# Three steps of the eighth pair put in another order: turning v, the coefficients of x, and a copy of half an expert

## The reference

```python
x = x + _L0_conv_ref(_gn(x), ...)   # shared + two chosen experts
x = x + _L1_conv_ref(_gn(x), ...)   # window attention + depthwise conv of v, projected
```

## Time and profile before

| | |
|---|---|
| median of three executions | 763.06 us (760.45 to 766.43) |
| profiled execution, its own time | 761.66 us |
| its span, first to last instruction | 759.7 us |
| PE busy | 645.3 us, 85% |
| DVE busy | 565.1 us, 74% |
| ACT busy | 453.1 us, 60% |
| POOL busy | 188.5 us, 25% |
| mean granted TensorE clock | 0.963 of full speed |

### The profile page before, as it was taken

One profiled execution on the slowest core, in us unless ns is written; L12 is line 12 of the kernel. 1 busy time (PEld: TensorE's weight loads), 2 busy tenths in 40 slices (PEclk: granted clock), 3 DMA queues, 4 the chain that ended last, 5 costly groups with the idle time before them and its releaser, 6 DMA issues.

```text
span 759.7 us, 18623 instructions
## 1 busy us (share of the span) xinstructions
PE 645.3 (85%) x6926; PEld 388.0 (51%) x6926; DVE 565.1 (74%) x1124; ACT 453.1 (60%) x758; POOL 188.5 (25%) x295
## 2 busy tenths in 40 slices
PE   5426759899989899999999899999999898889892
PEld 3412324655556464656555565646566566444430
DVE  3842656888888888988888888889888977332692
ACT  1123555768676776867686767768676852355451
POOL 4042133140404223131404042231312101000182
PEclk9997868999999999999999999999999999999997
DMA  8433183555646574746556464747452242465194
GB/s 329 180 132 98 59 223 108 174 158 153 184 129 200 145 206 147 213 128 200 160 151 189 128 199 144 215 138 210 134 168 86 82 147 72 139 222 181 20 257 167
DMA packets 53871, 121.13 MB, mean 159 GB/s; under 512 B 10131, under 2 KB 26646, under 8 KB 53782
## 3 DMA queue, kind: packets, MB, share of 16 engines
q1 hardware_dynamic: 41814, 78.87, 32.9%
q0 software_dynamic: 8800, 28.45, 15.3%
q10 hardware_dynamic: 3168, 12.62, 4.3%
HBM read 70.58 MB, written 40.93 MB: 147 GB/s over the span
## 4 chain that ended last, share of the span: by engine, by line
PE 47%; ACT 25%; issue 12%; DVE 6%; DMA 5%; POOL 1%; ACTq 1%; POOLq 1%; SPq 0%; DVEq 0%
PE g L1067 10%; PE g L1085 7%; ACT y L518 6%; PE t L1135 4%; PE g L1095 4%; PE g L1263 4%; ACT vp L563 4%; PE pv L1150 4%; PE s L1124 3%; PE s L1254 3%; DMA vt<-x 3%; ACT y L514 3%; ACT pt L584 3%; PE t L1254 3%; ACT L518 2%
## 5 line engine op out<-in xcount | busy, mean ns | idle before, releaser
L1067 PE MATMUL g<-xsh,wsel 96*128 96x512 f32 x256 | 132.6, 647 | 23.8 <-ACT y L514 13.1
L514 ACT ACTIVATE y<-g 128x512 f32<-128x512 f32 x96 | 55.6, 596 | 92.0 <-PE g L1067 75.6
L875 DVE TENSOR_REDUCE mx<-s 128x8 f32<-128x512 f32 x128 | 87.0, 679 | 26.8 <-PE s L1124 26.8
L811 DVE BATCH_NORM_STATS2 st<-y 128x6 f32<-128x512 f32 x96 | 64.6, 686 | 51.7 <-ACT y L514 51.6
L1135 PE MATMUL t<-ident,less 128*128 128x128 f32 x512 | 79.3, 278 | 15.7 <-ACT pt L584 15.0
L879 DVE TENSOR_TENSOR less<-s,mx 128x512 f32<-128x512 f32 x128 | 88.5, 691 | 4.4
L1067 PEld LDWEIGHTS g<-xsh,wsel 96*128 96x128 f32 x256 | 46.7, 200 | 76.3 <-issue 63.8
L1135 PEld LDWEIGHTS t<-ident,less 128*128 128x128 f32 x512 | 62.5, 145 | 44.7 <-DVE less L879 21.7
L584 ACT ACTIVATE pt<-t 128x512 f32<-128x512 f32 x128 | 74.6, 595 | 14.2 <-PE t L1135 13.7
L1150 PE MATMUL pv<-vp,pt 128*64 128x34 f32 x2048 | 79.2, 222 | 3.0 <-DVE ot L893 2.8
L1150 PEld LDWEIGHTS pv<-vp,pt 128*64 128x64 f32 x2048 | 71.4, 140 | 4.0 <-ACT pt L584 2.9
(11 more groups left out here) (155 smaller groups left out, 1119.7 us busy)
## 6 DMA issues: line engine op xcount, KB each, us to landing
xsh<-xs POOLq DMA_DIRECT2D x64, 210.0 KB, 3.7
xs<-xn ACTq DMA_DIRECT2D x16, 578.0 KB, 2.9
vt<-x SPq DMA_DIRECT2D x4, 2048.0 KB, 17.6
xin<-x POOLq DMA_DIRECT2D x16, 512.0 KB, 4.7
sq_d<-qhl SPq DMA_DIRECT2D x32, 256.0 KB, 2.4
sk_d<-khl SPq DMA_DIRECT2D x32, 256.0 KB, 2.2
stack<-sk_d SPq DMA_DIRECT2D x64, 128.0 KB, 3.5
stack<-sq_d SPq DMA_DIRECT2D x64, 128.0 KB, 2.8
```

The source lines that it names most:

```text
L514: act.activation(y[:, k, h * HALF:(h + 1) * HALF], g[at][:, :], ACT.Identity).then_inc(g_free[at], 1)
L811: last = v.bn_stats(st[:, 2 * k + h, :], y[:, k, h * HALF:(h + 1) * HALF])
L875: v.tensor_reduce(mx[:, p % 2, :], scored, AX.X, ALU.max).then_inc(sem["s_max"], 1)
L1067: last = mm(g[at][:, :], wsel[:, k - 1, C * dy:C * dy + C], xsh[:, k - 1, dy + 16 * h:dy + 16 * h + 16, 0:W], start=(dy == 0), stop=(dy == 1))
```

## The change

Three calls move within a turn; nothing is added or taken away.

1. On ACT in step 7 the copy of the second half of the first expert of image b+3 now stands ahead of `window(b + 2)`; before it stood behind it.
2. On DVE in step 7 `x_coefs(b + 2)` now stands ahead of `maxima`; before it stood behind it.
3. On DVE `turn_v(b + 1)` moves from the end of step 7 to the end of step 6, right behind `group_variance(b + 2, 1, 1)`.

```diff
@@ scalar, step @@
                     if p == 7:
+                        if has3:
+                            copy_y(b + 3, 1, (1,))
                         if has2:
                             window(b + 2)
-                        if has3:
-                            copy_y(b + 3, 1, (1,))
                         turn_out(b, 0)
@@ vector, step @@
+                    if has2 and p == 7:
+                        x_coefs(b + 2)
                     if has1 or p < PAIRS - 2:
                         maxima(b + (p + 2) // PAIRS, (p + 2) % PAIRS)
                     if has2 and p == 3:
                         y_coefs(b + 2)
-                    if has2 and p == 7:
-                        x_coefs(b + 2)
...
                         if has2:
                             group_variance(b + 2, 1, 1)
+                        if has1:
+                            turn_v(b + 1)
                     if p == 7:
                         if has3:
                             y_stats(b + 3, 1)
-                        if has1:
-                            turn_v(b + 1)
```

## The result

The changed kernel takes 772.64 us (median of four runs, 772.29 to 775.35) against 763.34 us for the kernel before (median of four, 760.45 to 766.43): 1.25% slower, ratio 1.0125 with an interval of 1.0089 to 1.0160. The profiled execution took 772.29 us with a span of 770.3 us; the one before took 761.66 with 759.7.

A forecast was written before the change was run, and what follows sets the result against it. It took PE, nearly full, and a chain of waits through PE, DVE, ACT and PE as the bound; 12 x 0.83 = +10.0 us, all else 0, gave 773.0 us on a median of 763.06, range 764 to 779.

The forecast's parts named there:

- The copy's term: On ACT ahead of the window, the copy waits for PE's matmul: k 0.83 us later in 12 turns, +10.0 us.
- The upper bound of the time, 776: Upper end of the total time with both bounds applied, 769.5 to 776 us.
- x_coefs and turn_v at nothing: On DVE, the coefficients come about when they did before, turn_v replacing the wait for the maxima: 0.
- The up to 0.3 us a turn that was to show without the copy: PE's wait for late outputs from DVE, covered while the copy makes PE wait anyway: up to 0.3 us a turn.
- the "on time" end of its bounds: DVE's outputs reach values on PE between on time, if DVE instructions overlap, and 0.3 us late.
- the forecast's bounds of -1.2 and +1.2: The last turns: turn 13 at +1.0 and turn 14 at -1.0 us, together 0, between -1.2 and +1.2.
- that window cost nothing, as forecast: In turn 12 the copy behind the window already waits 1.17 us for PE, more than 0.83: no cost.
- the wait of 1.0 us that the forecast put there: In turn 13, outputs on DVE end late for their reader on PE: +0.8 to +1.2, taken as +1.0 us.
- the forecast's -1.0 for `turn_v`: In turn 14 turn_v moves into a DVE idle hole, so the next maxima come earlier: -1.0 us (0 to -2.0).
- The copy that fills the hole: Rival: the copy is ready within ACT's 1.55 us wait for coefficients, up to 0.5 us saved a turn, 757 us; 5%.
- Nothing is given back behind k: Judges the rival that unseen slack in the turn gives the delay back, 763 to 769 us; 12%.
- The clock did not fall for PE's wait ahead of k: Judges the rival that PE's wait, grown from 0.32 to 1.15 us, drops the clock: 783 to 793 us; 6%.

The follow-up runs named there:

- coefficients, turn 14's `turn_v`: Kernel before with the coefficients ahead of the maxima, and turn_v at the end of step 6 only in turn 14: 754.38 us, ratio 0.9889.
- changed, expert earlier on PE: Changed kernel with the expert's second half ahead of values instead of behind it on PE in step 7: 766.45 us, ratio 1.0050 against the kernel before.

## Why the prediction was right, point by point

**The copy's term** was +0.83 us a turn and measured 35.63 - 34.80 = 0.83. Both halves of its reasoning stand in the rows: the hand-over from matmul to copy (363.62 + 1.98 to 365.70, 0.10 us; the prediction used 0.09) and the block's unchanged 5.84 us. The block is not quite "without a hole": ACT is idle for 0.47 us ahead of the second expert's copy, behind its own `normalise`. That is so in both kernels, so it leaves the term alone. The copy alone gives the whole term. The upper bound of the time, 776, is a little above the sum of its own terms, 773.0 + 1.0 + 1.2 = 775.2; nothing hangs on that.

**x_coefs and turn_v at nothing** was right. The up to 0.3 us a turn that was to show without the copy did not show: DVE's two moves alone made the turn 0.08 us shorter. In the changed kernel the coefficients came 364.70 - 363.62 = 1.08 us behind the start of PE's L1067; before, 361.36 - 360.14 = 1.22. The prediction had them slightly late, where they are 0.14 us early, because successive DVE instructions overlap: the coefficients' row starts at 364.55, while `turn_v` runs to 362.73 + 1.94 = 364.67. `outputs` ended at 366.64 and `values` ran at 366.88 without idle time, the "on time" end of its bounds. POOL's power took 0.57 us beside `turn_v`, as it did before, without `turn_v` beside it. The Trainium skill (SBUF — State Buffer, Who interferes with whom) has a VectorE instruction in a two-port mode and a GpSimd instruction shut each other out; this pair did not.

**The rest of the time** does not come in the places forecast, though it nearly cancels. PE's landmarks on the timelines, first of the kernel before, then of the changed one: k's first half of turns 0 and 1, the second half of q and k in turn 13, q and k at the start of turn 14, and the depthwise convolution:

```profile
124.10 1.13 PE L1085 MATMUL g<-xw,w 128*128 128x512 f32 x2 [1.03 <-ACT y L514]
...
158.43 1.12 PE L1085 MATMUL g<-xw,w 128*128 128x512 f32 x2 [0.32 <-ACT y L514]
...
579.88 2.03 PE L1085 MATMUL g<-xw,w 128*128 128x512 f32 x4
...
604.89 1.98 PE L1085 MATMUL g<-xw,w 128*128 128x512 f32 x4
...
654.76 4.80 PE L1254 MATMUL s<-vt,stack 64*32 64x512 f16 x112 [1.94 <-DVE stack L998]
```
```profile
123.01 1.13 PE L1085 MATMUL g<-xw,w 128*128 128x512 f32 x2 [1.02 <-ACT y L514]
...
157.76 1.13 PE L1085 MATMUL g<-xw,w 128*128 128x512 f32 x2 [1.28 <-ACT y L514]
...
588.24 2.03 PE L1085 MATMUL g<-xw,w 128*128 128x512 f32 x4
...
614.67 2.01 PE L1085 MATMUL g<-xw,w 128*128 128x512 f32 x4
...
662.25 4.80 PE L1254 MATMUL s<-vt,stack 64*32 64x512 f16 x112 [1.94 <-DVE stack L998]
```

| stretch | longer by, us | forecast |
|---|---|---|
| to the first k | -1.09 | 0 |
| turn 0, to k of turn 1 | +0.42 | +0.83 |
| to the second k of turn 13 | +9.03 | 11 x 0.83 = 9.13 |
| to the start of turn 14 | +1.42 | +1.0 |
| to the depthwise convolution | -2.29 | -1.0 |
| depthwise convolution to the end | +3.11 | 0 |
| sum | +10.60 | +10.0 |

That the sum lies so near the forecast is partly luck. The twelve turns of the copy gave 0.42 + 9.03 = 9.45 us, turns 13 to 15 -0.87 (inside the forecast's bounds of -1.2 and +1.2), and the two stages that the change does not touch -1.09 + 3.11 = +2.02.

The first row is the prologue, where no instruction moved; in the nine profiles the first k starts between 121.14 and 124.33 us. In turn 0 the clock fell in the kernel before and did not fall in the changed one, which hides half of that turn's loss: with DVE's two moves alone, where it did not fall either, the same stretch took 33.82 us, against 34.33 before. The +9.03 holds the window of turn 12 too, and is the worth of eleven turns, so that window cost nothing, as forecast.

For turn 13 here are rows of the changed kernel's timeline; then, by the columns of the earlier trace rows, the fourth and the fifth stretch of the table, first of the kernel before, with the place in the fifth where its clock fell, then of the changed one:

```profile
609.48 1.97 DVE L921 STREAM_TRANSPOSE vtmp<-vn 128x1024 f32<-128x1024 f32 x1
...
612.99 0.42 DVE L893 TENSOR_TENSOR ot<-pv,rec 128x256 f32<-128x256 f32 x1
...
613.72 1.01 PE L1150 MATMUL pv<-vp,pt 128*64 128x34 f32 x16
```
```profile
579.88:604.89 25.01, 21.48 (x248) 15.96 (x247) 22.59 (x49) 18.42 (x31) 1.41 (x2) 0.93 0.38 111
604.89:654.76 49.87, 41.73 (x513) 29.55 (x513) 34.57 (x59) 21.47 (x44) 6.33 (x4) 0.97 0.34 103
634.50:637.90 3.40, 3.40 (x34) 2.72 (x32) 0.96 (x2) 1.26 (x3) 0.00 (x0) 0.50 0.27 63
```
```profile
588.24:614.67 26.43, 22.93 (x249) 17.00 (x247) 23.36 (x50) 19.39 (x33) 4.49 (x4) 0.87 0.36 101
614.67:662.25 47.58, 40.14 (x516) 28.36 (x515) 34.03 (x57) 20.41 (x41) 3.26 (x3) 1.00 0.36 108
```

The same two stretches in all nine profiles, with the step in which `turn_v` stands and the granted clock:

| kernel | `turn_v` in turn 13 | turn 13, us | clock | `turn_v` in turn 14 | turns 14 and 15, us | clock |
|---|---|---|---|---|---|---|
| before | step 7 | 25.01 | 0.93 | step 7 | 49.87 | 0.97 |
| copy alone | step 7 | 24.97 | 0.93 | step 7 | 49.85 | 0.97 |
| copy and coefficients | step 7 | 24.92 | 0.93 | step 7 | 50.07 | 0.97 |
| coefficients alone | step 7 | 26.40 | 0.87 | step 7 | 48.56 | 1.00 |
| coefficients, turn 14's `turn_v` | step 7 | 26.10 | 0.87 | step 6 | 47.57 | 1.00 |
| changed | step 6 | 26.43 | 0.87 | step 6 | 47.58 | 1.00 |
| changed, expert earlier on PE | step 6 | 25.94 | 0.87 | step 6 | 47.57 | 1.00 |
| DVE alone | step 6 | 25.89 | 0.87 | step 6 | 48.67 | 0.96 |
| `turn_v` alone | step 6 | 26.69 | 0.94 | step 6 | 49.26 | 0.97 |

In turn 13 the order forecast is there, but `outputs` ends at 613.41 and PE reads it at 613.72 without idle time ahead: the wait of 1.0 us that the forecast put there does not stand in the row. The 1.42 us go with the clock. Five kernels had a clock of 0.87 over this stretch and took 25.89 to 26.43 us, two of them with `turn_v` still in step 7; three had 0.93 and took 24.92 to 25.01. (With `turn_v` alone the coefficients came late and the window waited 3.41 us.) Why the clock was low for longer in some kernels than in others stays open. In turns 14 and 15 the forecast's -1.0 for `turn_v` was right: at a clock of 1.00 the stretch takes 48.56 us with it in step 7 and 47.57 or 47.58 with it in step 6. The rest of the -2.29 is the clock, which was at 0.50, the 1.2 GHz level, for 3.40 us in the kernel before and did not fall there in the changed one: with `turn_v` in step 7 that is 49.87 against 48.56. The forecast left these changes of the clock out.

The last row, +3.11 us, is in a stage that the change does not touch. From the first depthwise matmul to the first of the last projection the same code took 58.4 us in the kernel before, 61.4 in the changed one and 57.2 to 60.6 in the seven experiments. The clock does not part the two kernels: it was 0.97 over this stage in both. No run ties the 3.0 us to the change: the changed kernel with one move on PE took 58.5 us there. What makes this stage vary was not found.

**The rivals.** The copy that fills the hole fails at the point it named: the copy starts 365.70 - 363.62 = 2.08 us behind the start of PE's L1067, where the block before started 361.38 - 360.14 = 1.24 us behind it, and bringing the matmul forward by one instruction group takes back 0.46 us. Nothing is given back behind k: the turn is longer by the whole term. The clock did not fall for PE's wait ahead of k, 1.28 us in the turn shown: from the first k of turn 0 to the second of turn 13, 123.01 to 588.24 us of the changed kernel, it was granted in full, 1.00.

## What to carry to other kernels

When an engine is idle ahead of a step on the critical path, another step may be pulled into the hole only if its own input is ready inside the hole; work out when it is ready from the producer's row before moving it, because everything behind it in the queue waits too. Two inputs of one block don't add: removing the earlier one gains nothing. Here the one part that took a dependency off the chain (the coefficients ahead of the maxima) made the kernel 1% faster by itself, and the two moves made along with it hid that, each by putting something else in the place that it had freed: `turn_v` ahead of the coefficients on DVE, the copy ahead of the window on ACT.

## What the runs showed of the hardware

The depthwise stage, the same instructions in all nine profiles, took from 57.2 to 61.4 us, four microseconds of scatter, nearly half of the effect looked for. The clock is a part of it at most: five profiles with a clock of 1.00 throughout took 57.2 to 59.0, four with 0.97 took 58.4 to 61.4. Turns in the middle of one profile repeat to within 0.04 us. A change of a few tenths of a microsecond a turn is read more surely from the turn's length in one profile than from the total, and stretches of two profiles are best compared where their granted clocks agree.
